# Attention from float32 products to three 16-bit products, with the steps of a sequence in another order

## The reference, cut to what matters

```python
# decayed linear attention, 32 heads of 64, 16 sequences of 256 tokens, width 256
qkv = silu(x @ qkv_w.T); q, k, v = split(qkv)
aw = (q @ k.T) * decay            # decay falls with distance, 0 above the diagonal
attn = rmsnorm(aw @ v, norm_w)
y = (sigmoid(x @ gate_w.T) * attn) @ out_w.T
x = layernorm(x + y)
# then a router (grouped top-k), 64 experts, 6 to a token, a shared expert
x = layernorm(x + moe(x) + shared(x))
```

## Time and profile before

| | |
|---|---|
| median of 3 runs | 1415.9 us (1414.46 to 1415.93) |
| the profiled execution, its own time | 1412.41 us |
| its span | 1410.4 us |
| PE busy | 1345.9 us, 95% |
| DVE busy | 894.6 us, 63% |
| ACT busy | 671.2 us, 48% |
| POOL busy | 366.5 us, 26% |
| granted TensorE clock, mean | 0.981 |

### The profile page before, as it was taken

The page is one execution under the profiler, slowest core; times in us unless marked ns, Lnnn a source line. Parts: engine busy times, 40 slices in busy tenths (PEclk is TensorE's granted clock), DMA queues, the critical chain, the costliest instruction groups (busy, mean ns, idle before and its releaser), DMA issues.

```text
span 1410.4 us, 36483 instructions
## 1 busy us (share of the span) xinstructions
PE 1345.9 (95%) x13995; PEld 1096.4 (78%) x13995; DVE 894.6 (63%) x2468; ACT 671.2 (48%) x1290; POOL 366.5 (26%) x422
## 2 busy tenths in 40 slices
PE   7999999999999999999999999999999999989960
PEld 5888888888888888888888888888888888865530
DVE  7856576666667575756576666667575756553337
ACT  8644454545454544445454545444444445433314
POOL 0212121212121122212121212121122222337754
PEclk9999999999999999999999999999999999999985
DMA  8500000000000000000000000000000000779957
GB/s 314 194 9 10 25 15 24 15 24 15 24 15 24 7 17 22 7 26 13 24 15 24 15 24 15 24 15 24 7 14 25 7 24 15 228 247 248 239 111 303
DMA packets 52962, 86.38 MB, mean 61 GB/s; under 512 B 6752, under 2 KB 32192, under 8 KB 52032
## 3 DMA queue, kind: packets, MB, share of 16 engines
q1 hardware_dynamic: 41728, 70.33, 14.7%
q0 software_dynamic: 5632, 8.26, 3.4%
q10 hardware_dynamic: 5568, 7.34, 1.5%
HBM read 60.08 MB, written 25.83 MB: 61 GB/s over the span
## 4 chain that ended last, share of the span: by engine, by line
PE 89%; DMA 4%; DVE 3%; issue 1%; POOL 1%; ACT 1%; SPq 0%; ACTq 0%; DVEq 0%; POOLq 0%
PE pA L467 25%; PE pB L467 23%; PE pC L543 13%; PE pO L557 12%; PE pS L529 10%; DMA sums<-sb_stage,sb_sidx 2%; PE pC L467 1%; PE pS L718 1%; DMA sb_W<-sums 1%; PE pC L577 1%; PE pB L701 1%; POOL sums L1292 0%; PE pS L701 0%; DVE sb_W L921 0%; DMA sb_stage<-gather_rows,sb_gidx 0%
## 5 line engine op out<-in xcount | busy, mean ns | idle before, releaser
L467 PE MATMUL pB<-sb_xh,sb_W 128*128 (+1 forms) x2048 | 349.9, 273 | 0.0
L1244 POOL TENSOR_TENSOR sb_fold<-sb_sq 128x256 f32<-128x256 f32 x128 | 111.5, 871 | 893.9 <-ACT sb_sq L801 893.9
L467 PE MATMUL pB<-sb_xl,sb_W 128*128 (+1 forms) x1024 | 279.3, 273 | 0.0
L467 PEld LDWEIGHTS pB<-sb_xh,sb_W 128*128 128x128 f16 x2048 | 200.5, 98 | 23.8 <-issue 0.2
L799 ACT ACTIVATE sb_yh<-sb_y 128x512 f16<-128x512 f32 x128 | 80.6, 630 | 286.4 <-DVE sb_y L937 286.4
L543 PE MATMUL pC<-sb_S,sb_v 128*64 128x256 f32 (+1 forms) x2048 | 194.7, 332 | 0.0
L945 DVE TENSOR_TENSOR sb_ql<-sb_q,sb_qh 128x512 f16<-128x512 f32 x128 | 88.0, 687 | 167.7 <-ACT sb_qh L775 164.3
L774 ACT ACTIVATE sb_q<-pA 128x512 f32<-128x512 f32 x128 | 76.4, 597 | 223.2 <-PE pA L467 223.1
L467 PE MATMUL pA<-sb_xh,sb_W 128*128 (+1 forms) x1024 | 175.9, 274 | 5.7 <-DVE sb_W L921 5.7
L467 PE MATMUL pA<-sb_W,sb_xh 128*128 128x256 f16 x1024 | 177.0, 275 | 2.1 <-ACT sb_qh L775 2.1
L557 PE MATMUL pO<-sb_Wo,sb_yh 128*128 128x256 f16 x1024 | 174.7, 273 | 1.0 <-DVE sb_yl L941 1.0
(11 more groups left out here) (210 smaller groups left out, 2315.5 us busy)
## 6 DMA issues: line engine op xcount, KB each, us to landing
sb_stage<-wprep SPq DMA_DIRECT2D x7, 1280.0 KB, 6.6
sb_W<-sums SPq DMA_DIRECT2D x16, 512.0 KB, 11.1
sb_W<-w_experts SPq DMA_DIRECT2D x16, 384.0 KB, 5.4
gather_rows<-sb_xr SPq DMA_DIRECT2D x16, 320.0 KB, 2.3
sb_D<-w_experts SPq DMA_DIRECT2D x12, 384.0 KB, 4.4
sb_xs<-xT SPq DMA_DIRECT2D x17, 256.0 KB, 2.9
sb_D<-decay SPq DMA_DIRECT2D x8, 512.0 KB, 7.6
sb_xn<-x SPq DMA_DIRECT2D x16, 256.0 KB, 3.0
```

The lines of the kernel that those rows point to most:

```text
L467: last = nc.tensor.matmul(dst, a, m, start=(i == 0), stop=(i == len(terms) - 1), **kw)
L1244: nc.gpsimd.tensor_tensor(fold[:, :], sq[:, 0:T], sq[:, T:2 * T], ALU.add).then_inc(s_fold, 1)
```

## The change

`attention` becomes three passes of 16-bit operands, 24 matmuls in place of 8. For it ACT makes the upper parts of S (`high_S`, two instructions) and of v (`high_v`), and DVE their lower parts (`low_S`, one instruction over 128x1536 elements, and `low_v`, 128x512). `decayed` is done for all four heads at once, in two instructions in place of four. On TensorE the order of a step becomes q, scores, k, attention, v, output, gate; `output` is that of g-3 in place of g-2; the pieces for the sequence before are placed elsewhere. DVE, ACT and POOL get a new order to match. The buffer for early units of the shared expert moves into the weights' staging buffer, two constants into xr, and the decay loads use two semaphores in place of eight. In the last pass the units of the shared expert are spread otherwise.

```diff
@@ sync
             def load_decays(Q):
-                sp.dma_start(D[:, Q, :], decay[Q]).then_inc(s_decay[Q], 16)
+                wait(sp, s_decay[Q % 2], 16 * (Q // 2))
+                sp.dma_start(D[:, Q, :], decay[Q]).then_inc(s_decay[Q % 2], 16)
@@ tensor
             def attention(q, h):
-                pe.wait_ge(s_Sm, 2 * h + 2)
-                pe.wait_ge(s_ve, h + 1)
+                pe.wait_ge(s_Sl, h + 1)
+                pe.wait_ge(s_vl, h + 1)
                 wait(pe, s_sq, h)
+                wait(pe, s_y, h)
                 i = q % 2
+                products = [(vh[i], Sh), (vl[i], Sh), (vh[i], Sl)]
                 for u in range(2):
-                    for t in range(NT):
-                        for e in range(2):
-                            head = 2 * u + e
-                            last = nc.tensor.matmul(pC[64 * e:64 * e + 64, u * T + t * P:(u + 1) * T],
-                                                    v32[i][:, t, head * HD:(head + 1) * HD],
-                                                    S[:, head, 0:T] if t == 0 else S[:, head, T:T + P],
-                                                    start=(t == 0), stop=(t == NT - 1))
+                    for t, (a, z_) in enumerate(HALVES):
+                        for n, (v, s) in enumerate(products):
+                            for e in range(2):
+                                head = 2 * u + e
+                                last = nc.tensor.matmul(pC[64 * e:64 * e + 64, u * T + t * P:(u + 1) * T],
+                                                        v[:, t, head * HD:(head + 1) * HD], s[:, head, a:z_],
+                                                        start=(t == 0 and n == 0), stop=(t == NT - 1 and n == len(products) - 1))
                 last.then_inc(s_C, 1)
...
                 if has(g):
                     project_q(b, q, g)
-                    project_k(b, q, g)
                 if has(g - 1):
                     scores((q - 1) % NQ, g - 1)
+                if behind(b):
+                    if q == 2:
+                        sum_squares(b, g - 2)
+                    if q == 4:
+                        router(b)
+                    if q == 6:
+                        count(b, g - 2)
+                if has(g):
+                    project_k(b, q, g)
+                if tail and q == 1:
+                    output(b, (q - 3) % NQ, g - 3)
                 if has(g - 2):
                     bank_of_attention(b, q)
                     attention((q - 2) % NQ, g - 2)
...
                 if has(g):
                     project_v(b, q, g)
+                if has(g - 3) and not (tail and q == 1):
+                    output(b, (q - 3) % NQ, g - 3)
+                if has(g):
                     project_gate(b, q, g)
-                if has(g - 2):
-                    output(b, (q - 2) % NQ, g - 2)
-                if behind(b):
-                    piece(b, q, g - 1)
...
+                if behind(b) and q == 3:
+                    transpose_rows(b, g - 1)
@@ scalar
             def act_v(q, g):
                 act.wait_ge(s_v, g + 1)
+                wait(act, s_vl, g)
+                nc.scalar.activation(v32[:, :, :].rearrange("p t n -> p (t n)"), pA[:, :], ACT.Silu,
+                                     scale=1 / W_SCALE).then_inc(s_ve, 1)
+
+            def high_v(q, g):
+                act.wait_ge(s_ve, g + 1)
                 wait(act, s_C, g - 1)
-                nc.scalar.activation(v32[q % 2][:, :, :].rearrange("p t n -> p (t n)"), pA[:, :], ACT.Silu,
-                                     scale=1 / W_SCALE).then_inc(s_ve, 1)
+                nc.scalar.activation(vh[q % 2][:, :, :], v32[:, :, :], ACT.Copy).then_inc(s_vh, 1)
+
+            def high_S(h, i):
+                act.wait_ge(s_Sm, 2 * h + i + 1)
+                wait(act, s_C, h)
+                a, z_ = HALVES[i]
+                nc.scalar.activation(Sh[:, :, a:z_], S[:, :, a:z_], ACT.Copy).then_inc(s_Sh, 1)
...
                 if has(g):
                     act_k(q, g)
...
-                if has(g - 2):
-                    act_y(g - 2)
+                if has(g - 1):
+                    high_S(g - 1, 0)
                 if has(g):
                     act_v(q, g)
+                if has(g - 1):
+                    high_S(g - 1, 1)
+                if has(g - 2):
+                    squares(g - 2)
+                    high_y(g - 2)
+                if has(g):
...
                     act_gate(q, g)
+                if behind(b) and q == 3 and not tail:
+                    evacuate_x1(b)
+                if has(g):
+                    high_v(q, g)
@@ vector
-            def decayed(b, q, h, u):
-                dve.wait_ge(s_S, 2 * h + u + 1)
...
+            def decayed(b, q, h):
+                dve.wait_ge(s_S, 2 * h + 2)
...
+                nc.vector.tensor_tensor(S[:, :, 0:T], pS[:, :, 0:T], d, ALU.mult).then_inc(s_Sm, 1)
+                nc.vector.tensor_tensor(S[:, :, T:T + P], pS[:, :, T:T + P], d[:, :, 0:P], ALU.mult).then_inc(s_Sm, 1)
+
+            def low_S(h):
+                dve.wait_ge(s_Sh, 2 * h + 2)
+                nc.vector.tensor_tensor(Sl[:, :, :], S[:, :, :], Sh[:, :, :], ALU.subtract).then_inc(s_Sl, 1)
+
+            def low_v(q, g):
+                dve.wait_ge(s_vh, g + 1)
+                wait(dve, s_C, g - 1)
+                nc.vector.tensor_tensor(vl[q % 2][:, :, :], v32[:, :, :], vh[q % 2][:, :, :], ALU.subtract).then_inc(s_vl, 1)
...
                 if behind(b):
                     if q == 2:
                         norm_sums(b)
+                    if q == 3:
                         residual(b)
                     if q == 4:
                         low_x1(b)
-                        route_scores(b)
                     if q == 5:
                         route_groups(b)
-                        route_experts(b)
                     if q == 6:
                         running_counts(b)
-                        search(b)
-                    if q == 7:
-                        fill_slots(b)
-                        route_weights(b)
...
+                if has(g - 1):
+                    low_v((q - 1) % NQ, g - 1)
+                    decayed(b, (q - 1) % NQ, g - 1)
+                if behind(b):
+                    if q == 3:
+                        statistics(b)
+                    if q == 4:
+                        route_scores(b)
+                    if q == 5:
+                        route_experts(b)
+                if has(g - 2):
+                    gate((q - 2) % NQ, g - 2)
                 if has(g):
                     low_q(q, g)
...
+                if behind(b) and q == 3:
+                    normed(b)
                 if has(g):
                     low_k(q, g)
...
+                if behind(b) and q == 6:
+                    search(b)
                 if has(g - 1):
-                    decayed(b, (q - 1) % NQ, g - 1, 0)
+                    low_S(g - 1)
                 if has(g - 2):
                     low_y(g - 2)
...
+                if behind(b) and q == 7:
+                    fill_slots(b)
+                    route_weights(b)
@@ gpsimd
-                if q == 3 and not last_b:
+                if q == 5 and not last_b:
                     split_tokens(b + 1)
```

More of the change, by code:

```diff
@@ L147, in block_kernel @@
         kl = [sb(f"kl{i}", [P, 2, T], F16) for i in range(2)]
[L148 removed]
+        v32 = sb("v32", [P, NT, QH * HD])
+        vh = [sb(f"vh{i}", [P, NT, QH * HD], F16) for i in range(2)]
+        vl = [sb(f"vl{i}", [P, NT, QH * HD], F16) for i in range(2)]
         gt = [sb(f"gt{i}", [P, 2 * T]) for i in range(2)]
         S = sb("S", [P, QH, T + P])
+        Sh = sb("Sh", [P, QH, T + P], F16)
+        Sl = sb("Sl", [P, QH, T + P], F16)
         y32 = sb("y32", [P, 2 * T])
@@ L243, in block_kernel @@
         late = 2 * in_w * PAIR_W
-        units = [xe[:, j, :] for j in range(UNIT_EARLY)]
+        xe = flat.bitcast(F16)
+        units = [xe[:, j * 2 * NC * T:(j + 1) * 2 * NC * T] for j in range(UNIT_EARLY)]
         units += [W[:, late + j * 2 * NC * T:late + (j + 1) * 2 * NC * T] for j in range(SEQS - 1 - UNIT_EARLY)]
@@ L272, in block_kernel @@
         s_stage = [sem(f"s_stage{i}") for i in range(2)]
-        s_decay = [sem(f"s_decay{i}") for i in range(NQ)]
+        s_decay = [sem(f"s_decay{i}") for i in range(2)]
         s_wh, s_wl = sem("s_wh"), sem("s_wl")
@@ L561, in output @@
                 last.then_inc(s_D, 1)
[L563 to L589, removed]
@@ new lines, in bank_free, with sum_squares, transpose_rows @@
+            def bank_free(attended):
+                wait(pe, s_sq, attended)
+                wait(pe, s_y, attended)
+            def sum_squares(b, attended):
+                bank_free(attended)
+                pe.wait_ge(s_acc, 8 * b)
+                for t in range(NT):
+                    last = group(pC[:, t:t + 1], [(acc[:, t * P:(t + 1) * P], ones[:, 0:1])])
+                last.then_inc(s_ss, 1)
```

(29 more changed lines are left out.)

108 lines of the change are left out of this document (56 added, 52 removed).

## The result

The changed kernel takes 1459.6 us (median of 4 runs, 1458.5 to 1461.7) against 1415.2 for the kernel before: a ratio of 1.0318, 95% interval 1.0300 to 1.0335. It is slower, as forecast, but by 44 us where 14 were forecast, and it lies above the range, whose ends were 1392 and about 1450. The profiled execution took 1461.7 with a span of 1459.7, 49.3 more than the span before.

The account below looks back on a forecast made before the run. TensorE bounds the kernel before; after the change a circle through DVE and TensorE sets the period. 1412.4 + 6 (loop) + 7 (sequence 0) + 1 (drain) = 1426.4, on the median about 1430; range 1392 to about 1450.

Parts of the forecast that it names:

- the cost on TensorE: TensorE's steps: attention falls from 1.45 to 1.10 us, a step to 8.97, a sequence on TensorE alone to 73.8.
- Rival B: Attention on TensorE is held by its weight loads: 1450 us (chance 0.10), or about 1590 if nothing overlaps (0.03).
- POOL's holds: Each POOL fold or acc holds a DVE instruction with two SBUF inputs for about 0.54 us, twice a step.
- Rival A: POOL's additions cost DVE nothing, or lag has more room; TensorE stays the bound: 1392 us, chance 0.22.
- my timetable: One sequence drawn up with predicted durations: DVE runs without a gap from step 2 to `running_counts` in step 6, 35.5 us.
- the period: Time of one looped sequence: 76.05 us against 75.66, +0.4 for each of 15 sequences, +6 us in all.
- The circle through DVE: DVE's gapless stretch in steps 2 to 6, 35.5 us, then TensorE's remaining steps; together 76.05 us a sequence.
- sequence 0: First sequence, where DVE also splits weights and its steps run over TensorE's: +7 us, bounds 0 and 12.
- the drain: After the last looped sequence: last gate about 0.5 us later and squares ahead of y's upper part, 0.5 more: +1 us.

Follow-up runs that it names:

- the two runs that took the holds away: Changed kernel with POOL's two additions of squares shrunk to 2 columns: 1436.3 us; changed kernel with these additions moved beside `decayed`: 1433.9 us.
- the run with the early unit loads: Changed kernel with SP issuing the shared expert's three early unit loads ahead of the last looped sequence's row store and the last token load: 1456.2 us.
- the lengthened body: Kernel before, still looped, with 8 one-column matmuls added at the head of each step's first projection: 1492.1 us, measured one time.

## Why the prediction was right and wrong

**Right: the cost on TensorE.** Attention at 1.11 and a period of TensorE alone at 73.86, forecast as 1.10 and 73.8. Rival B did not come: L558's weight loads take 0.110 and hide. The rule that I set against the rows there, of the Trainium skill (TensorEngine Tiling (Array Packing), "Restrictions and Gotchas"), is that column tiling excludes fast weight load. A load of 64 columns in attention does take 0.110, where one of 128 columns in `scores` takes 0.094 to 0.095; whether the rule is the reason no run here shows. At 24 loads in pairs it costs no time here.

**Right: POOL's holds, their size and number.** Seven holds of 0.53 (forecast 0.54) in a DVE stretch of 35.4 (forecast 35.5). Rival A asked that they be free; the two runs that took the holds away show what that would have been: 23 and 26 us less, with DVE's instructions at their plain lengths. One detail was wrong: POOL does not get in at each boundary. At 509.67 `fold` waited through `low_k`, `low_S` and `low_y`; it got its hold in front of `low_x1`, two instructions later than in my timetable, and `acc` followed in front of `low_v`, so the sum was the same.

**Right in the mechanism, 0.46 high: the period.** The circle through DVE in steps 2 to 6 and TensorE in the rest gave 76.05; with the stall of the return taken out by the written-out program it is 75.59. The longer circle through DVE uses up TensorE's gain against 75.66. On this alone the looped part would have cost nothing, where I had +6.

**Right in the number: sequence 0**, forecast +7, measured 9.0 less the 2.5 of placement, 6.5. The steps of that sum were not followed in the trace, and the run with the early unit loads, whose sequence 0 is the same program, has it 1.5 shorter.

**Wrong: the step that costs the longer program of TensorE at nothing.** The change adds 64 matmuls and as many weight loads to the loop body; I counted their time in the pairs and nothing for having them. The return to the loop's head then costs 2.26 each, 31.7 us for 14 in the profiled execution and 29.5 by the medians. That 14 and 30 make just the 44 measured is luck: without the returns the kernel would have taken 1430.0, the very time forecast, but with a looped part some 7 lower and a drain some 10 higher than I had them. The page of before gave a hint that I left unread: the instruction queue with 20 packets for a program that goes through its body 15 times, where the written-out one moves 111. That is a body that is fetched once.

**Wrong in size: the drain**, +11.7 where I wrote +1. I followed DVE's chain and the new places of the units on TensorE, and not SP's queue: the unit loads stand behind a store that waits for the work which DVE now does last and late. Taking this away gave 5.8 of the drain back; the waits of 2.36 and 2.43 us for DVE's last products that then appear are most of the rest. SP's queue could have been read before the change.

The sum of the profiled execution is thus: looped part without returns -1 (forecast +6), returns +31.7 (none), sequence 0 +6.5 (+7), drain +11.7 (+1), the end +0.4 (0), together 49.3. That is 5 over the excess of the medians.

## What to carry to other kernels

When a change lengthens the program of an engine inside a hardware loop, look at the packets of the instruction queue and at what stands at the loop's head: here a body that had been kept lost about 2 us at each return once it was too long, and more where TensorE's clock fell behind the standing; writing the loop out gave that back. When work moves to DVE, list which of its instructions read two SBUF operands, and put POOL's instructions beside those that read PSUM; here even a wait added to POOL's queue paid. An exact timetable of the steady loop says nothing about loop heads, first and last sequences: read there each DMA queue for what stands behind the late engine's last product.

## What the runs showed of the hardware that I had not expected

TensorE's program with 16 sequences of 8 steps, looped, needs 20 instruction packets with 24 + 16 matmul instructions for scores and attention in a step, and 147 with 24 + 24; (147 - 20) / 14 is about 9 packets a return. Written out, 119 packets run without a stall at the same place, and 111 in the kernel before: fetching straight ahead hides, returning does not. How long a body may be was not measured, only that the kernel before lies below and the changed one above.

The stall isn't constant: 1.65 to 2.22 in the changed kernel, 2.18 to 2.78 in the kernel before with the lengthened body. Behind some of the returns the granted clock falls to half, 1.2 GHz (2 of 14 in the changed kernel, 11 of 14 in the lengthened one), and such a period is some 1.8 and 1.7 us longer. In the loops without a stall, those of the kernel before and of both kernels written out, it stays at 1.00.

A POOL addition of 256 columns holds a DVE instruction with two SBUF inputs for 0.53 of its 0.73 us, whichever instruction of DVE it is, 512 or 1536 columns long; and POOL may itself wait through three of DVE's, 3.27 us for an instruction of 0.73.
